# First GRU step's router projection behind the gates, distance rows loaded on SyncE, identity matmuls around the ends' spreading

## The chip, the core and the metric

The kernel runs on one core of a Trainium2 chip. The core has TensorE (PE, matmuls into PSUM), VectorE (DVE), ScalarE (ACT), GpSimd (POOL) and SyncE (SP, which here only issues transfers), each with its own instruction stream; they meet through semaphores. Sixteen DMA engines move data. The metric is the device time of one launch in microseconds, all four stages of the block together.

## What is computed

A block of four sublayers over `x` (32 batches, 100 rows, 256 features) with a context of 32 x 361 x 256, each added to `x` through a gate:

```python
x = x + tanh(g_xattn[0]) * cross_attention(layernorm(x), ctx)
x = x + tanh(g_ffn[0])   * gru_routed_mixture(layernorm(x))
x = x + tanh(g_xattn[1]) * align(ctx, layernorm(x))
x = x + tanh(g_ffn[1])   * capacity_experts(layernorm(x))
```

The change touches the second and the third. In the second a GRU of state width 1024 runs over the 100 rows of each batch, and its states route each row to experts; beside it a projection `expr` of the inputs is needed for the router's scores:

```python
def step(h, xw_t):
    xr, xz, xn = split(xw_t, 3); hr, hz, hn = split(h @ gru_w_hh.T, 3)
    r = sigmoid(xr + hr); z = sigmoid(xz + hz)
    n = tanh(xn + r * hn)
    return (1 - z) * n + z * h
expr = hidden_states @ expr_w.T
```

In the third each batch gets the Euclidean distances of its 100 normalized rows to its 361 context rows, a dynamic time warping over them, the path back, and for each row of `x` the sum of the context rows on the path:

```python
D = sqrt(maximum(aa + bb - 2 * a @ b.T, 0))
R = dtw_cost(D); i_idx, j_idx, valid = backtrack(R)
out = zeros.at[j_idx].add(small[i_idx] * valid)
```

## The kernel before

The order of every engine's work is written out by hand: each engine has a block of code per stage, and an engine's instructions run in the order in which they are written. Semaphore waits (`wait_ge`) stand in the engine's own stream, so whatever is queued behind one waits too.

**The GRU (`gru`).** All 32 batches advance together, 100 steps in 25 tiles of four (`STEPS`); the state is kept as 128 partitions (four quarters of the features by 32 batches). TensorE's step, from L1048 on: input parts of the gates (L1053, into `ps_rz`) and of the candidate (L1058, into `ps_x`), two transposes of the state (L1062), then for the quarter `j` of the tile the router projection (L1064 to L1071, weights `we`, into `ps_e`), then the recurrent gate matmuls (L1076, which need the turned state, copied to `stateT` by VectorE at L999 and ScalarE at L1028) and the recurrent candidate matmuls (L1081). Between the transposes and the gate matmuls the projection covers the copies. Each f32 matmul is two passes in the trace, hence 64 records for 32 matmuls. The weights `we` (1 MB) are loaded by SyncE at the stage's start (L964).

**The distances (`distances`).** Loop over 32 batches, groups of four for the rows' statistics. SyncE loads the first four batches' rows of `x` in two halves and then the contexts `ctxT[b]` (363 KB each) into a ring of eight buffers; from the ninth on it waits until the buffer's squares and distances are done. ScalarE waits for the second half of the first rows, issues the other seven row loads (L1866), and then starts with the square root of the first group's variances (`root_of(0)`, L1852). In its loop it squares context `b`, takes the root for the next group, squares row `b`, and takes the root of distance `b - 2`. VectorE: statistics (L1891 to L1896), reciprocal (L1901), normalized rows (L1907), then per batch `take_x` (L1912), at every fourth batch the statistics of the next group, the rows two batches ahead, and the distance of two batches ago (L1917). GpSimd adds the two halves of the squares. TensorE transposes the rows (L1950) and does three matmuls for each batch. After the loop the distances are placed into `table`.

**The ends (`align`).** VectorE finds the path in `DSTEPS` = 106 steps of two instructions (L2193, L2198), each raising the semaphore `own`. TensorE stands still through this. When `own` is at its end it spreads the path's ends of group 0 and group 1 over the partitions (`spread_ends`, four matmuls each, L2392). ScalarE copies each group out (L2352), VectorE makes three pick tables of each (L2208, L2211, `pick_ready`), and the loop over groups follows: TensorE waits for the picks, spreads group `g + 2`, and selects for each batch with three matmuls (L2428) into `ps_e[b % 3]`; VectorE adds each result to `rows` (L2216). `fill_tensor_engine` (L209 to L212) issues matmuls of the identity whose results nobody reads; the kernel before has seven of them at L2448 and seven at L2542.

## Time and profile before

| | us |
|---|---|
| median of 3 runs | 3206.34 (3204.51 to 3207.49) |
| the profiled execution | 3209.85 |
| its span in the trace | 3208.1 |
| TensorE busy | 2880.4 (90%) |
| VectorE, ScalarE, GpSimd busy | 1310.6, 827.8, 811.1 |
| GRU, first instruction of step 0 to the last state | about 650 to 2080 |
| distances | 2587 to 2691 |
| forward and backward pass of the path | to 2885.8 |

The profile is one execution. A timeline row gives the start, the time from the first start to the last end of like instructions in a row, the engine, the line, output and inputs, and in brackets how long the engine had been idle before and what ended that. TensorE's granted clock is given per stretch as a share of 2.4 GHz; its two levels are 1.0 (2.4 GHz) and 0.5 (1.2 GHz). Times in the trace count from the start of the span.

### The profile page before, as it was taken

Reading aid. Unit: us, or ns where it says so; the run is one execution under the profiler, and the core shown is the slowest. Engines: PE = TensorE matmul, PEld = TensorE weight load, DVE = VectorE, ACT = ScalarE, POOL = GpSimd, SP = SyncE. Lnnn points to the kernel's source line nnn. Section 1 sums busy time; section 2 is a strip of 40 time slices with the busy share of each in tenths; the row PEclk is TensorE's granted clock in tenths of the full one; section 3 lists DMA queues with packets and bytes.
Section 4 is the critical chain, followed back from the end, with each engine's and each line's share of the span. In section 5 each row is a group of like instructions: output and inputs, shape, how many; then the busy total and the mean of one; then the engine's idle time right before and its main releaser. Section 6 shows DMA issues by size and latency. Waiting matters only on the chain. (4 is left out here: it accounts for less than half of the span.)

```text
span 3208.1 us, 70894 instructions
## 1 busy us (share of the span) xinstructions
PE 2880.4 (90%) x29244; PEld 1559.8 (49%) x29245; DVE 1310.6 (41%) x2655; ACT 827.8 (26%) x2170; POOL 811.1 (25%) x759
## 2 busy tenths in 40 slices
PE   7999999899999999999999999999999974009898
PEld 4566666534444444444444444478566643007555
DVE  5655555613332323323323233264222256986311
ACT  3444444411111111111111111121222246471111
POOL 2111111002222222222222222234444431004243
PEclk9999999999999999999999999999999988559899
DMA  7000100220000000000000000051222263005143
GB/s 239 30 26 26 32 26 26 71 81 23 18 23 18 19 22 18 23 17 21 19 18 25 16 24 16 18 205 47 43 45 45 44 175 98 0 1 206 52 116 75
DMA packets 78391, 164.11 MB, mean 51 GB/s; under 512 B 11788, under 2 KB 51568, under 8 KB 73111
## 3 DMA queue, kind: packets, MB, share of 16 engines
q1 hardware_dynamic: 53588, 104.04, 10.4%
q0 software_dynamic: 21456, 40.57, 5.7%
q10 hardware_dynamic: 3074, 15.45, 1.3%
q8 instruction: 223, 3.65, 0.5%
q14 instruction: 50, 0.40, 0.0%
HBM read 119.63 MB, written 40.37 MB: 50 GB/s over the span
## 5 line engine op out<-in xcount | busy, mean ns | idle before, releaser
L1076 PE MATMUL gru_ps_rz<-whh,scratch 128*32 128x512 f32 x6400 | 709.3, 595 | 0.0
L871 POOL TENSOR_TENSOR scratch<-scratch 128x1024 f32<-128x1024 f32 (+3 forms) x246 | 369.5, 1527 | 818.8 <-DVE stat L885 656.5
L1076 PEld LDWEIGHTS gru_ps_rz<-whh,scratch 128*32 128x32 f32 x6400 | 197.9, 110 | 454.1 <-issue 454.1
L1081 PE MATMUL gru_ps_n<-whh,scratch 128*32 128x256 f32 x6400 | 363.6, 379 | 0.0
L1005 DVE TENSOR_TENSOR scratch<-scratch,state 128x256 f32<-128x256 f32 x100 | 52.2, 522 | 667.4 <-ACT scratch L1034 667.4
L1081 PEld LDWEIGHTS gru_ps_n<-whh,scratch 128*32 128x32 f32 x6400 | 207.7, 110 | 180.2 <-issue 59.9
L467 DVE TENSOR_REDUCE att_neg_max<-att_banks 100x2 f32<-100x722 f32 x256 | 221.1, 906 | 122.6 <-PE att_banks L701 122.6
L1034 ACT ACTIVATE scratch<-gru_ps_rz 128x512 f32<-128x512 f32 x100 | 59.7, 597 | 726.7 <-PE gru_ps_rz L1076 726.7
L390 ACT ACTIVATE att_probsT<-att_banks 121x600 f32<-121x600 f32 x256 | 154.3, 672 | 216.7 <-PE att_banks L744 216.7
L1053 PE MATMUL gru_ps_rz<-wih,scratch 128*32 128x512 f32 x1600 | 191.7, 597 | 1.7 <-POOL scratch L973 1.7
L2392 PE MATMUL e_ps_g<-align_reach,ident 32*121 32x101 f32 x64 | 10.9, 326 | 197.0 <-DVE align_reach L2198 195.5
L885 DVE TENSOR_REDUCE stat<-scratch 128x2048 f32 (+3 forms) x96 | 181.1, 1886 | 0.0
L1007 DVE TENSOR_TENSOR scratch<-scratch,gru_ps_n 128x256 f32<-128x256 f32 x100 | 42.1, 421 | 230.3 <-PE gru_ps_n L1081 230.3
L1037 ACT ACTIVATE scratch<-scratch 128x256 f32<-128x256 f32 x100 | 41.7, 417 | 349.0 <-DVE scratch L1009 349.0
L355 POOL DMA_DIRECT2D x<-rows_x x31 | 17.3, 559 | 418.9 <-DVE rows_x L493 418.9
L701 PE MATMUL att_banks<-att_kT,att_qT 32*100 32x361 f32 x1024 | 111.9, 506 | 9.5 <-ACT att_probsT L390 9.1
L744 PE MATMUL att_banks<-att_q_less,att_kT 32*121 32x100 f32 x3072 | 108.7, 277 | 10.8 <-DVE att_neg_max L467 9.5
L1622 DVE COPY mix_room<-mix_ps_m 128x512 f32<-128x512 f32 x57 | 39.4, 692 | 187.7 <-PE mix_ps_m L1711 187.7
L1297 POOL DMA_INDIRECT x<-mix_room,mix_rows_listed x57 | 90.4, 1585 | 90.6 <-ACT mix_room L1357 87.8
L744 PEld LDWEIGHTS att_banks<-att_q_less,att_kT 32*121 32x121 f32 x3072 | 93.6, 179 | 35.9 <-issue 25.0
L1703 PE MATMUL mix_ps_g<-whh,mix_room 128*128 x228 | 107.3, 593 | 2.3 <-ACT mix_room L1351 2.3
L1717 PE MATMUL mix_ps_y<-whh,mix_room 128*128 x456 | 108.0, 380 | 1.0 <-DVE mix_room L1622 1.0
(400 smaller groups left out, 4237.8 us busy)
## 6 DMA issues: line engine op xcount, KB each, us to landing
table<-in_w SPq DMA_DIRECT2D x16, 1024.0 KB, 6.9
states<-state SPq DMA_DIRECT2D x100, 128.0 KB
scratch<-states SPq DMA_DIRECT2D x25, 512.0 KB, 3.5
whh<-in_whhT POOLq DMA_DIRECT2D x8, 1536.0 KB, 19.9
att_c_in<-in_ctxT SPq DMA_DIRECT2D x32, 363.0 KB, 3.2
dist_ctx<-in_ctxT SPq DMA_DIRECT2D x32, 363.0 KB, 4.6
align_ctx<-in_ctx_rows SPq DMA_DIRECT2D x32, 363.0 KB
whh<-in_guT ACTq DMA_DIRECT2D x8, 1024.0 KB, 12.3
```

The source lines that it names most:

```text
L390: nc.scalar.activation(probsT[(HG * b + c) % RING][:, 2 * h:2 * h + 2, :], pair(TURNED, c, h)[0:KC, :, 0:3 * S], ACT.Exp, scale=-1.0).then ...
L467: v_.tensor_reduce(neg_max[0:S, g, :].rearrange("p (r j) -> p r j", j=32)[:, 2 * h:2 * h + 2, HD * (1 - half)], pair(SCORES, c, h)[0:S, :, ...
L701: done = nc.tensor.matmul(banks[0:S, bank_of(SCORES, c, r), 0:KV], qT[b % 2][strip(r), half, g, :], kT[b % 2][strip(r), half, g, 0:KV], st ...
L744: done = nc.tensor.matmul(banks[0:KC, bank_of(TURNED, c, r), m * S:(m + 1) * S], kT[b % 2][strip(r), half, g, m * KC:(m + 1) * KC], q_less ...
L871: done = nc.gpsimd.tensor_tensor(last.prod[:, row:row + rows, :], a, b, ALU.mult)
L885: nc.vector.tensor_reduce(stat[:, bass.ds(it, 1), at:at + rows].rearrange("p a n -> p (a n)"), last.prod[:, 0:rows, :], AX.X, ALU.add).the ...
L1053: nc.tensor.matmul(ps_rz[quarter(q), :], xt[u][:, k, j, :], rz_columns(wih, k, q), start=(k == 0), stop=False)
L1076: last = nc.tensor.matmul(ps_rz[quarter(q), :], stateT[c % 2][:, quarter(c // 2)], rz_columns(whh, c, q), start=False, stop=(c == GC - 1))
L1081: last = nc.tensor.matmul(ps_n[quarter(q), 0:GQ], stateT[c % 2][:, quarter(c // 2)], n_columns(whh, c, q), start=(c == 0), stop=(c == GC - 1))
L1297: nc.gpsimd.indirect_dma_start(x2, bass.IndirectOffsetOnAxis(ap=rows_listed[:, n:n + 1], axis=0), y[u], None, compute_op=ALU.add).then_inc ...
L1703: done = nc.tensor.matmul(psum[:, :], xT[u][:, k, :], experts_w[:, bass.ds(e, 1), k * 2 * FF + half * FF:k * 2 * FF + (half + 1) * FF].rea ...
L1717: done = nc.tensor.matmul(ps_y[:, 0:DIM], midT[:, c, :], experts_w[:, bass.ds(e, 1), GU + c * DIM:GU + (c + 1) * DIM].rearrange("p a n -> ...
```

## The change

Three edits, and no change in what is computed.

1. In the GRU the router projection moves into a helper `project_routed`. It is called where it stood in every step but the very first (`t == 0`); there it is called behind the recurrent gate matmuls.
2. In the distances SyncE issues all row loads, each for a group of four batches: group 0 ahead of the contexts, group `g` behind context `2g - 1`. ScalarE issues none and does not wait for the first rows; it runs a root of one column of `ones` into `warm` at its start, which loads the table of the root. VectorE waits for each group's single load.
3. In `align` TensorE waits until `own` is 16 short of its end (eight steps of two), runs four identity matmuls into `ps_e[2]`, then spreads groups 0 and 1, and runs four more.

```diff
@@ -1043,6 +1043,16 @@
             pe.wait_ge(whh_in, 16 * GC)
             pe.wait_ge(wih_in, 16)
 
+            def project_routed(it, u, j):
+                if j == 0:
+                    pe.wait_ge(we_in, 16)
+                if j % 2 == 0:
+                    pe.wait_ge(e_copied, 2 * it)
+                for k in range(KT):
+                    last = nc.tensor.matmul(ps_e[j // 2][:, (j % 2) * GQ:(j % 2 + 1) * GQ], xt[u][:, k, :, :].rearrange("p j b -> p (j b)"),
+                                            we[:, k, j * GQ:(j + 1) * GQ], start=(k == 0), stop=(k == KT - 1))
+                last.then_inc(e_done, 1)
+
             def steps(it, u):
                 pe.wait_ge(xt_ready, it + 1)
                 for j in range(STEPS):
@@ -1061,14 +1071,8 @@
                     for half in range(2):
                         nc.tensor.transpose(ps_t[half][:, 0:P], h[j % 2][:, half * P:(half + 1) * P], ident[:, :]).then_inc(turned, 1)
 
-                    if j == 0:
-                        pe.wait_ge(we_in, 16)
-                    if j % 2 == 0:
-                        pe.wait_ge(e_copied, 2 * it)
-                    for k in range(KT):
-                        last = nc.tensor.matmul(ps_e[j // 2][:, (j % 2) * GQ:(j % 2 + 1) * GQ], xt[u][:, k, :, :].rearrange("p j b -> p (j b)"),
-                                                we[:, k, j * GQ:(j + 1) * GQ], start=(k == 0), stop=(k == KT - 1))
-                    last.then_inc(e_done, 1)
+                    if t > 0:
+                        project_routed(it, u, j)
                     for half in range(2):
                         pe.wait_ge(stateT_ready[half], t + 1)
                     for c in range(GC):
@@ -1076,6 +1080,8 @@
                             last = nc.tensor.matmul(ps_rz[quarter(q), :], stateT[c % 2][:, quarter(c // 2)], rz_columns(whh, c, q),
                                                     start=False, stop=(c == GC - 1))
                     last.then_inc(rz_done, 1)
+                    if t == 0:
+                        project_routed(it, u, j)
                     for c in range(GC):
                         for q in range(4):
                             last = nc.tensor.matmul(ps_n[quarter(q), 0:GQ], stateT[c % 2][:, quarter(c // 2)], n_columns(whh, c, q),
@@ -1802,13 +1808,13 @@
         ps_d = [ps(f"ps_d{u}") for u in range(RING)]
 
         rows_in = [sem(f"rows_in{g}") for g in range(GROUPS)]
-        first_in = [sem(f"first_in{u}") for u in range(2)]
         ctx_in = [sem(f"ctx_in{u}") for u in range(CTX)]
         padded, squared, added = sem("padded"), sem("squared"), sem("added")
         stats_done, aggregated, root_in, root_out, scaled = (sem("stats_done"), sem("aggregated"), sem("root_in"), sem("root_out"),
                                                              sem("scaled"))
         xn_ready, turned, xT_ready, norm_ready = sem("xn_ready"), sem("turned"), sem("xT_ready"), sem("norm_ready")
         ones_done, summed, square_ready, dist_ready = sem("ones_done"), sem("summed"), sem("square_ready"), sem("dist_ready")
+        warm, warmed = sb("warm", [S, 1]), sem("warmed")
         far_set, placed, taken = sem("far_set"), sem("placed"), [sem("taken_act"), sem("taken_dve")]
         block = ctx.enter_context(nc.Block())
 
@@ -1822,13 +1828,18 @@
 
         @block.sync
         def _(sp):
-            for some, arrived in ((slice(0, 2), first_in[0]), (slice(2, GROUP), first_in[1])):
-                sp.dma_start(rows[:, some, :], x_rows[:, some, :]).then_inc(arrived, 16)
+            def load_rows(g):
+                some = slice(GROUP * g, GROUP * g + GROUP)
+                sp.dma_start(rows[:, some, :], x_rows[:, some, :]).then_inc(rows_in[g], 16)
+
+            load_rows(0)
             for b in range(B):
                 if b >= CTX:
                     sp.wait_ge(squared, b - CTX + 1)
                     sp.wait_ge(summed, b - CTX + 1)
                 sp.dma_start(c_in[b % CTX][:], ctxT[b]).then_inc(ctx_in[b % CTX], 16)
+                if b % 2 and b // 2 + 1 < GROUPS:
+                    load_rows(b // 2 + 1)
 
         @block.gpsimd
         def _(pool):
@@ -1860,10 +1871,8 @@
                 act.wait_ge(square_ready, b + 1)
                 nc.scalar.activation(dist[:, b, 0:KV], dist[:, b, 0:KV], ACT.Sqrt).then_inc(dist_ready, 1)
 
-            act.wait_ge(first_in[1], 16)
-            for g in range(1, GROUPS):
-                some = slice(GROUP * g, GROUP * g + GROUP)
-                act.dma_start(rows[:, some, :], x_rows[:, some, :]).then_inc(rows_in[g], 16)
+            nc.scalar.activation(warm[:], ones[0:S, 0:1], ACT.Sqrt).then_inc(warmed, 1)
+            act.wait_ge(warmed, 1)
             root_of(0)
             for b in range(B + LEAD):
                 if b < B:
@@ -1883,11 +1892,8 @@
 
             def stats_of(g):
                 some = slice(GROUP * g, GROUP * g + GROUP)
-                if g > 0:
-                    dve.wait_ge(rows_in[g], 16)
+                dve.wait_ge(rows_in[g], 16)
                 for b in range(GROUP * g, GROUP * g + GROUP):
-                    if g == 0:
-                        dve.wait_ge(first_in[b // 2], 16)
                     v.bn_stats(stats[:, b, :], rows[:, b, :]).then_inc(stats_done, 1)
                 for b in range(GROUP * g, GROUP * g + GROUP):
                     dve.wait_ge(stats_done, b + 1)
@@ -2413,8 +2419,11 @@
                                             start=(k == 0), stop=(k == KT - 1))
                 done.then_inc(scored, 1)
 
+            pe.wait_ge(own, POINTERS + 2 * DSTEPS - 16)
+            fill_tensor_engine(nc, ps_e[2], ident, 4)
             spread_ends(0)
             spread_ends(1)
+            fill_tensor_engine(nc, ps_e[2], ident, 4)
             for g in range(GROUPS):
                 pe.wait_ge(pick_ready, 3 * g + 3)
                 if g + 2 < GROUPS:
```

In the order of TensorE, start of the GRU (`gru_ps_rz` holds the gates, `gru_ps_e` the projection, `gru_ps_n` the candidate); a name of the kernel before comes first. Before:

```order
L1053 MATMUL gru_ps_rz<-wih,scratch 32x512 x8
L1058 MATMUL gru_ps_x<-wih,scratch 32x256 x8
L1062 MATMUL gru_ps_t<-ident,state 128x128 x2
L1069 MATMUL gru_ps_e<-gru_we,scratch 128x256 x2
L1076 MATMUL gru_ps_rz<-whh,scratch 32x512 x32
L1081 MATMUL gru_ps_n<-whh,scratch 32x256 x32
L1053 MATMUL gru_ps_rz<-wih,scratch 32x512 x8
L1058 MATMUL gru_ps_x<-wih,scratch 32x256 x8
```

and after:

```order
L1063 MATMUL gru_ps_rz<-wih,scratch 32x512 x8
L1068 MATMUL gru_ps_x<-wih,scratch 32x256 x8
L1072 MATMUL gru_ps_t<-ident,state 128x128 x2
L1080 MATMUL gru_ps_rz<-whh,scratch 32x512 x32
L1052 MATMUL gru_ps_e<-gru_we,scratch 128x256 x2
L1087 MATMUL gru_ps_n<-whh,scratch 32x256 x32
L1063 MATMUL gru_ps_rz<-wih,scratch 32x512 x8
L1068 MATMUL gru_ps_x<-wih,scratch 32x256 x8
```

In the first step the two projection matmuls now stand between gates and candidate; the second step is as before.

ScalarE at the start of the distances (`dist_rstd` is the variance that becomes the reciprocal root), before:

```order
L1866 DMA rows<-x 100x1024 x7
L1852 ACT_TABLE_LOAD
L1852 ACTIVATE dist_rstd<-dist_rstd 100x4
L1847 ACTIVATE dist_square<-dist_ctx 128x722
L1852 ACTIVATE dist_rstd<-dist_rstd 100x4
L1857 ACTIVATE dist_xx,dist_norm<-dist_xn 100x256
```

and after:

```order
L1874 ACT_TABLE_LOAD
L1874 ACTIVATE dist_warm<-ones 100x1
L1863 ACTIVATE dist_rstd<-dist_rstd 100x4
L1858 ACTIVATE dist_square<-dist_ctx 128x722
L1863 ACTIVATE dist_rstd<-dist_rstd 100x4
L1868 ACTIVATE dist_xx,dist_norm<-dist_xn 100x256
```

The seven issues are gone and the table load stands at the start, ahead of the first root.

SyncE at the same place, before:

```order
L1823 UNCONDITIONAL_BRANCH
L1826 DMA rows<-x 100x512 x2
L1831 DMA dist_ctx<-in_ctxT 128x726 x32
L1780 UNCONDITIONAL_BRANCH
L2128 UNCONDITIONAL_BRANCH
```

and after:

```order
L1833 DMA rows<-x 100x1024
L1840 DMA dist_ctx<-in_ctxT 128x726 x2
L1833 DMA rows<-x 100x1024
L1840 DMA dist_ctx<-in_ctxT 128x726 x2
L1833 DMA rows<-x 100x1024
L1840 DMA dist_ctx<-in_ctxT 128x726 x2
L1833 DMA rows<-x 100x1024
```

One row load of four batches now stands behind each second context, up to eight in all.

TensorE around the ends (`e_ps_g` takes the spread ends, `e_ps` the selections), before:

```order
L1979 MATMUL dist_ps_x<-ident,dist_all 32x100 x364
L1780 UNCONDITIONAL_BRANCH
L2381 UNCONDITIONAL_BRANCH
L2392 MATMUL e_ps_g<-align_reach,ident 121x101 x12
L2428 MATMUL e_ps<-align_ctx,align_cost 100x256 x12
L2392 MATMUL e_ps_g<-align_reach,ident 121x101 x4
```

and after:

```order
L1985 MATMUL dist_ps_x<-ident,dist_all 32x100 x364
L1786 UNCONDITIONAL_BRANCH
L2387 UNCONDITIONAL_BRANCH
L212 MATMUL e_ps<-ident 128x512 x4
L2398 MATMUL e_ps_g<-align_reach,ident 121x101 x8
L212 MATMUL e_ps<-ident 128x512 x4
L2398 MATMUL e_ps_g<-align_reach,ident 121x101 x4
L2437 MATMUL e_ps<-align_ctx,align_cost 100x256 x12
```

Four identity matmuls now stand ahead of the first eight spreads, and four between these and the spread of group 2.

## Rows read from the trace of the kernel before

**Rows 1.** The page, busy time of the engines over the span.

```profile
PE 2880.4 (90%) x29244; PEld 1559.8 (49%) x29245; DVE 1310.6 (41%) x2655; ACT 827.8 (26%) x2170; POOL 811.1 (25%) x759
```

**Rows 2.** Timeline, GRU step 0: start us, us, engine, line, what [idle <-releaser].

```profile
655.38 0.27 ACT L1028 COPY scratch<-gru_ps_t 128x128 f32<-128x128 f32 x1 [7.03 <-PE gru_ps_t L1062]
...
658.58 2.07 PE L1069 MATMUL gru_ps_e<-gru_we,scratch 128*128 128x256 f32 x4 [3.23 <-DMA gru_we<-in_weT]
660.58 8.98 PE L1076 MATMUL gru_ps_rz<-whh,scratch 128*32 128x512 f32 x64
669.39 3.63 PE L1081 MATMUL gru_ps_n<-whh,scratch 128*32 128x256 f32 x64
...
675.80 1.03 PE L1069 MATMUL gru_ps_e<-gru_we,scratch 128*128 128x256 f32 x4
676.76 7.07 PE L1076 MATMUL gru_ps_rz<-whh,scratch 128*32 128x512 f32 x64
```

**Rows 3.** Windows, step 0: stretch, us, PE busy, granted clock, DMA share, GB/s.

```profile
656.00:658.00 2.00, 0.00 (x0) 0.91 0.87 340
...
664.00:666.00 2.00, 2.00 (x24) 0.88 0.00 0
```

**Rows 4.** Timeline, all engines, start of the distances.

```profile
2591.22 3.76 ACTq L1866 DMA_DIRECT2D rows<-x  x7
2591.22 0.75 DVE L1891 BATCH_NORM_STATS2 dist_stats<-rows 100x6 f32<-100x256 f32 x2 [0.42 <-DMA rows<-x]
...
2595.01 1.28 ACT L1852 ACT_TABLE_LOAD   x1 [14.23 <-issue]
...
2596.54 0.18 DVE L1901 RECIPROCAL dist_rstd<-dist_rstd 100x4 f32<-100x4 f32 x1 [4.08 <-ACT dist_rstd L1852]
...
2597.86 0.37 DVE L1912 TENSOR_SCALAR dist_xT<-dist_ps_x 128x200 f32<-128x200 f32 x1 [0.37 <-PE dist_ps_x L1950]
2600.56 1.40 DVE L1891 BATCH_NORM_STATS2 dist_stats<-rows 100x6 f32<-100x256 f32 x4 [2.33 <-DMA rows<-x]
```

**Rows 5.** Context loads and squares of all; the third load; DMA queues 2600 to 2602.

```profile
L1847 ACT ACTIVATE dist_square<-dist_ctx x32: 788/790/794, 2596.4 to 2664.0; 128x722 f32<-128x722 f32 x32
...
L1831 SPq DMA_DIRECT2D dist_ctx<-in_ctxT x1: 427/427/427, 2588.9 to 2588.9; - x1
...
DMA to landing us min/median/max: 6.3/6.3/6.3
...
q10 hardware_dynamic: 67, 0.25, 37.1%
q1 hardware_dynamic: 70, 0.19, 27.9%
```

**Rows 6.** Timeline, all engines, around the ends' spreading.

```profile
2880.33 0.32 DVE L2193 SCALAR_TENSOR_TENSOR align_masked<-align_place,align_reach,table 128x91 f16<-128x91 f16 x1
...
2885.86 3.57 PE L2392 MATMUL e_ps_g<-align_reach,ident 32*121 32x101 f32 x16 [195.52 <-DVE align_reach L2198]
2887.84 0.50 ACT L2352 CAST align_ends<-e_ps_g 121x404 f16<-121x404 f32 x1 [2.73 <-PE e_ps_g L2392]
...
2890.95 1.94 PE L2392 MATMUL e_ps_g<-align_reach,ident 32*121 32x101 f32 x8 [1.53 <-DVE align_cost L2211]
...
2900.12 1.08 PE L2392 MATMUL e_ps_g<-align_reach,ident 32*121 32x101 f32 x8
2900.23 0.48 DVE L2216 SCALAR_TENSOR_TENSOR rows<-e_ps,gate_x,rows 100x256 f32<-100x256 f32 x1 [0.48 <-PE e_ps L2428]
...
2901.14 4.13 PE L2428 MATMUL e_ps<-align_ctx,align_cost 121*100 121x256 f32 x18
```

**Rows 7.** The later fill: matmuls, weight loads, and a window with the granted clock.

```profile
2978.48 8.07 PE L212 MATMUL e_ps_g<-ident 128*128 128x512 f32 x14
...
2979.47 0.34 PEld L212 LDWEIGHTS e_ps_g<-ident 128*128 128x128 f32 x1 [0.52 <-issue]
...
2982.00:2983.00 1.00, 1.00 (x4) 0.94 0.00 0
```

## The prediction

> **What bounds the kernel now.** TensorE is busy for 90% of the span [rows 1], so the first question for each edit is whether TensorE, or what it waits for, is late at that place. I read the timeline of the first GRU step, then of the start of the distances, then of the stretch in which the path's ends are spread, with the granted clock beside each. All three are single passages, run once, in a chain where each stage starts when the one ahead has ended. Time taken out of one is taken out of the kernel unless a later wait holds an absolute time; I found none: the later waits are on work of the same chain and move with it.
>
> **Part 1, the first GRU step.** Before, TensorE turns the state, and the next thing in its queue is the router projection, which needs the weights `we`. It sits idle for 3.23 us until their DMA lands at 658.58 [rows 2]. The turned state had been ready from 655.38 + 0.27 = 655.65 on. The granted clock had come up to full by then, falls during the idle time (0.91 over 656 to 658) and is back only in 664 to 666 [rows 3]. So the wait costs twice: the projection takes 2.07 us instead of the 1.03 of the next step, and the 64 recurrent gate passes 8.98 instead of 7.07 [rows 2].
> With the projection behind the gate matmuls of step 0 only, these start when the state is there, about 0.35 us after TensorE went idle:
> - idle time: 3.23 - 0.35 = 2.9 us less;
> - gate matmuls at full clock: 8.98 - 7.07 = 1.9 us less;
> - the projection is still run, at full clock and behind the gates: 2.07 - 1.03 = 1.0 us less. By 662.8 its weights have long landed (658.58).
> Sum 5.8 us. What is late next? The sigmoids start when the gates end and now have the projection and the candidate matmuls (1.0 + 3.5 us) as cover instead of 3.5 alone, so they hold nobody. The copy of the projection is taken in step 2 and is far off. From the end of the candidate matmuls on the step is as before. The bounds: 2.9 us if the clock falls or rises late all the same (the idle time alone), 5.8 with the clock up. I take 5.8, since the 0.35 us of idle that stays is about what TensorE shows in every later step with its clock up.
>
> **Part 2, the start of the distances.** Before, ScalarE waits for both halves of the first rows (2591.22), then issues seven row loads (3.76 us), then loads the root's table at 2595.01 (1.28 us), and only then takes the root that VectorE needs at 2596.54 [rows 4]. After, VectorE waits for one load of the four first batches. Its end I put where the second half landed, 2591.22. Four statistics (1.40), then aggregation and the epsilon (about 0.35 more, an estimate: they are shorter than the statistics and overlap them in part), root (0.2) with hand-overs (0.1): the reciprocal at 2593.2, that is 3.3 us earlier. The table load lies at the stage's start at 2587.3, where ScalarE has nothing else. But what holds the stage is the next wait: VectorE has taken batch 0 at 2597.86 + 0.37 and then stands until the second group of rows lands, at 2600.56 [rows 4]; everything behind follows from that moment. After, it would be there at 2598.23 - 3.3 = 2594.9. So the gain is decided by when the second group lands, now the fourth transfer of SyncE's queue, behind the first rows and contexts 0 and 1, instead of the first of ScalarE's, issued at 2591.22.
> Its landing time: the third context, issued at 2588.9, landed 6.3 us later, at 2595.2 [rows 5], behind 0.40 MB of rows and with 3 x 0.363 MB of contexts. In 2600 to 2602, with transfers outstanding in both queues, these took only 37.1 + 27.9 = 65% of the 16 DMA engines' time [rows 5]. So something like a third of the engines have no part in the rows' transfers, and I count each 0.40 MB of rows as 0.615 MB. Then 0.615 + 1.09 = 1.70 MB had landed at 2595.2. I put the first packets at 2588.5, 1.2 us after SyncE's first issue at the stage's start, and 1.4 us for the completion (both estimates; the one row load whose issue and landing the rows bound, 2587.3 to 2591.22, leaves room for them), so the rate is 1.70 / 5.3 = 0.32 MB/us. The second group ends at 2 x 0.615 + 2 x 0.363 = 1.96 MB, or 6.1 us: 2588.5 + 1.4 + 6.1 = 2596.0. With plain bytes (1.53 MB against 1.49) it would be 2595.3. I take 2596.2: 4.3 us gained. Bounds: 5.6 if VectorE itself is last (2594.9), 3.3 if the landing slips to 2597.3.
> The Trainium skill (page "DMA: Bandwidth & Descriptors", section "Why a DMA increments its semaphore by 16 and not by 1") says that a transfer over 100 partitions is put on 10 of the 16 engines, one over 128 on all. The 65% above agrees. With that page's figure of about 27 GiB/s for an engine the four transfers would take an estimated 4.3 us and land before 2594.9, which would make this part 5.6 us and the time 3192.7; the landing of 6.3 us measured here says that the engines are slower than that.
> SyncE then queues eight more issues than before, each some 0.4 us, without a wait up to context 7; that is far ahead of their use.
>
> **Part 3, around the ends.** Before, the spreads of groups 0 and 1 run at half clock: 16 passes in 3.57 us from 2885.86, where eight later ones take 1.08 [rows 6]. After, four identity matmuls are released eight VectorE steps before the path's end, at 2880.35 (the row at 2880.33 is the first of the eight). A matmul here is two passes, each 0.34 + 0.52 = 0.86 us at half clock; in the fill of seven at 2978.48 the clock came up 3.6 us after its start, and the passes took half of that from there [rows 7]. So: 3.6 us for 4.2 passes, then 3.8 x 0.43 = 1.6, end at 2885.6, just ahead of the path's end at 2885.86. Then at full clock: two spreads 2 x 1.02 = 2.0 (2887.9), the second fill 8 x 0.43 = 3.4 (2891.35), third spread 1.0 (2892.4). The second fill is in the way: the picks would release the third spread at 2890.95 - 0.85 = 2890.1, so it costs 1.2 us. Then four selections at (4.13 / 3) each = 5.4 us with the hand-over: the fourth result is added at 2897.8 instead of 2900.23 [rows 6]. Gain 2.4 us. VectorE is busy without a break from that addition on (statistics, then the picks of group 2), so this shift carries. If the clock comes up only after 5.5 us the first fill ends 0.7 late: 1.7 us. I take 2.2; bounds -1 and 3.5.
>
> **Sum.** 5.8 + 4.3 + 2.2 = 12.3 us. The profiled execution took 3209.85 us (span 3208.1), 3.5 above the median of the three runs; it gives 3197.6 for the same execution, and the median 3206.34 - 12.3 = **3194.0 us**.
>
> **Rivals.**
> - *The clock is no gain in the GRU step* (it falls, or rises late, also without the wait). Against it: the clock is still at 0.91 on average over 656 to 658 after the wait has begun, and only 0.35 us of idle is left. Part 1 is 2.9: 3196.9. Chance 0.12.
> - *The fills are in the way.* The clock stays low through both: first fill 6.9 us (2887.25), spreads 3.4, second fill 6.9, third spread 1.9, four selections as before 7.4: 2906.8 instead of 2900.23, 6.6 lost. Gain 10.1 - 6.6 = 3.5: 3202.8. Against it: fills brought the clock up within 3.6 us. Chance 0.04; for part 3 at about zero (3196.2) another 0.1.
> - *The row loads starve the contexts*, on the other side. Context 15 is needed at 2632.0 before (the last of the 32 squares at 2664.0, and 2.0 us for each one ahead of it, a little under the mean of (2664.0 - 2596.4) / 31 = 2.2 with the slow start in it [rows 5]), 2627.7 after. Ahead of its end SyncE's queue then holds all rows: 8 x 0.615 + 16 x 0.363 = 10.7 MB. At 0.32 MB/us that is there at 2623.2, 4.5 us to spare. At 0.25 it comes at 2632.7 and takes back 5.0 (3199.0, chance 0.06). From 0.215 MB/us down it costs more than the 12.3 us of all three parts; at 0.18 it comes at 2649.3, 21.6 late: 3194.0 + 21.6 = 3215.6. For it: all loads now share one queue, and rows crowd on part of the engines. Against it: the rate measured at the start. Chance 0.02.
> - *The change does less than it says*: the second rows land as late as 2600, since contexts and rows interleave. Part 2 is then 0.5: 3197.8. Chance 0.06.
>
> **How the numbers follow.** My forecast has 0.6. Of the rivals those at 3196 to 3199 hold 0.34 and stay faster; 0.04 for two of them at once, taken out of that, the low clock through the fills (0.04) lie within 0.2%. The low end: 5.8 + 5.6 + 3.5 = 14.9, or 3191.4, and 1.5 us for the spread of the median: 3190. The high end takes in one rival of the larger kind, 3200. Range **3190 to 3200**. A measurement of this kernel can tell about 0.2%, 6.4 us, from no change, so the line of "faster" is 3199.9: faster 0.90, same 0.08, slower 0.02.
>
> **What would show it.** Step 0: gate matmuls start near 655.7, take 7.1 us, and no idle time waits for `we`. Distances: reciprocal some 6 us after the stage's start, the second group's statistics 8.9 us after it instead of 13.3, and a steady 2.0 us per batch behind, with no wait on a context. Ends: clock up at the first spread, the fourth addition some 12 us after the path's end instead of 14.4, and the third spread waiting for the fill rather than for the picks. The forecast is wrong if the clock is low in the gates of step 0, if squares wait for contexts, or if the fills are still at half clock when the path ends.

## The result, and the profile after

| | before | changed |
|---|---|---|
| median of 11 runs each | 3206.97 us (3203.97 to 3216.10) | 3199.68 us (3193.61 to 3202.51) |
| ratio | | 0.9974, 95% interval 0.9965 to 0.9983 |
| the profiled execution, its span | 3209.85, 3208.1 | 3199.82, 3198.1 |

The changed kernel is faster by 5.5 to 11 us, 8.3 by the ratio, where I had forecast 12.3. Two later comparisons of the same two kernels gave 0.9963 (0.9950 to 0.9977) and 0.9965 (0.9952 to 0.9977), 11 to 12 us. So the direction and the range held, the range in the first comparison by 0.3 us (3199.68 against its end at 3200); the medians of the later two are 3194.94 and 3195.69 us. The question is where the difference to 12.3 sits.

The first GRU step, TensorE's timeline of the changed kernel (start and duration in us, engine, line, operation, out<-in, count, and in brackets the idle time ahead of it with what ended it), against [rows 2]:

```profile
649.54 3.33 PE L1063 MATMUL gru_ps_rz<-wih,scratch 128*32 128x512 f32 x16 [1.73 <-POOL scratch L973]
...
654.56 7.08 PE L1080 MATMUL gru_ps_rz<-whh,scratch 128*32 128x512 f32 x64 [0.45 <-ACT scratch L1028]
661.56 1.13 PE L1052 MATMUL gru_ps_e<-gru_we,scratch 128*128 128x256 f32 x4
662.62 3.66 PE L1087 MATMUL gru_ps_n<-whh,scratch 128*32 128x256 f32 x64
666.10 1.90 PE L1063 MATMUL gru_ps_rz<-wih,scratch 128*32 128x512 f32 x16
```

The wait for `we` is gone, the gates take 7.08 us instead of 8.98, the projection 1.13 instead of 2.07. From the step's first matmul to that of the next step it is 16.56 us, before 22.6.

The start of the distances, all engines, against [rows 4]:

```profile
2584.39 1.28 ACT L1874 ACT_TABLE_LOAD   x1 [6.68 <-PEq L1107]
...
2589.34 1.41 DVE L1897 BATCH_NORM_STATS2 dist_stats<-rows 100x6 f32<-100x256 f32 x4 [14.37 <-DMA rows<-x]
...
2591.56 0.18 DVE L1907 RECIPROCAL dist_rstd<-dist_rstd 100x4 f32<-100x4 f32 x1 [0.33 <-ACT dist_rstd L1863]
...
2592.87 0.37 DVE L1918 TENSOR_SCALAR dist_xT<-dist_ps_x 128x200 f32<-128x200 f32 x1 [0.37 <-PE dist_ps_x L1956]
2593.91 1.41 DVE L1897 BATCH_NORM_STATS2 dist_stats<-rows 100x6 f32<-100x256 f32 x4 [0.67 <-DMA rows<-x]
```

The stage starts at 2584.39. The table load lies in idle time, the reciprocal comes 7.2 us after the start, and the second group's statistics 9.52 us after it, before 13.28. The last wait there is still the landing of those rows (0.67 us of idle).

Around the path's ends, TensorE, against [rows 6]:

```profile
2877.52 2.09 PE L212 MATMUL e_ps<-ident 128*128 128x512 f32 x4
2879.54 1.93 PE L2398 MATMUL e_ps_g<-align_reach,ident 32*121 32x101 f32 x16
2881.40 3.71 PE L212 MATMUL e_ps<-ident 128*128 128x512 f32 x8
2885.05 1.08 PE L2398 MATMUL e_ps_g<-align_reach,ident 32*121 32x101 f32 x8
```

Both spreads together take 1.93 us instead of 3.57, the second fill ends as the third spread starts, and from the path's end (2879.41) to the fourth addition it is 12.1 us instead of 14.4.

So each passage shows what the prediction named, with sizes that are compared with it further down. What I had not looked for stands elsewhere. At the first expert tile of the mixture, 1590 us behind the GRU's first step and in code that the change doesn't touch, TensorE in the changed kernel shows

```profile
2240.35 3.78 PE L1709 MATMUL mix_ps_g<-whh,mix_room 128*128 x4 [1.62 <-ACT mix_room L1357]
```

and in the kernel before

```profile
2246.44 1.98 PE L1703 MATMUL mix_ps_g<-whh,mix_room 128*128 x4 [1.79 <-ACT mix_room L1351]
```

The windows of TensorE show what the clock did (stretch, its length, TensorE busy and its matmuls, the granted clock, the DMA share, GB/s); first the changed kernel, then the one before at the same work:

```profile
2238.00:2240.00 2.00, 0.41 (x2) 0.91 0.45 131
2240.00:2242.00 2.00, 1.65 (x2) 0.50 0.15 35
2242.00:2244.00 2.00, 2.00 (x4) 0.50 0.08 31
2244.00:2246.00 2.00, 2.00 (x4) 0.50 0.00 0
2246.00:2248.00 2.00, 1.45 (x5) 0.88 0.00 0
```

```profile
2244.00:2246.00 2.00, 0.41 (x2) 1.00 0.47 131
2246.00:2248.00 2.00, 1.56 (x4) 1.00 0.13 29
2248.00:2250.00 2.00, 2.00 (x6) 1.00 0.10 37
```

Both have the same pauses of TensorE there, between the shared expert's last matmuls and the first gates. Before, the clock stays at 2.4 GHz through them; after, it falls to 1.2 GHz and comes back some 7 us later. The tile takes 13.49 us instead of 10.63: 2.9 us given back.

### The profile page after: what moved, and what is told of

Same layout as the page of the kernel before. It is cut to its first block and busy times, and to the rows that moved or that the text cites. A ratio compares the mean times of both kernels' runs of the same rounds, so it can differ in the third digit from the quotient of the medians.

```text
span 3198.1 us, 70927 instructions
## 1 busy us (share of the span) xinstructions
PE 2887.9 (90%) x29260; PEld 1563.9 (49%) x29261; DVE 1309.8 (41%) x2655; ACT 828.2 (26%) x2171; POOL 811.7 (25%) x759
## 5 line engine op out<-in xcount | busy, mean ns | idle before, releaser
L212 PE MATMUL e_ps<-ident 128*128 128x512 f32 x16 | 9.4, 739 | 190.1 <-DVE align_reach L2204 190.1
L1037 ACT ACTIVATE scratch<-scratch 128x256 f32<-128x256 f32 x100 | 41.7, 417 | 350.3 <-DVE scratch L1009 350.3
## 6 DMA issues: line engine op xcount, KB each, us to landing
whh<-in_guT ACTq DMA_DIRECT2D x8, 1024.0 KB, 12.3
```

## The experiments

Behind the first two runs twelve more were made, so there are 14 traces of ten different kernels (three of the changed kernel, two each of the kernel before and of the GRU part alone). Each passage of the table is measured between the same two instructions in every trace. "GRU 0": first input matmul of step 0 to that of step 1. "Tile": from the transposing of the first expert tile's tokens to that of the third tile's, which takes in all matmuls of the first tile's gate and up projections. "Distances": the stage's start to the first matmul that places distances in the table. "Ends": the path's end to the fourth addition. "Tail": the last addition to the capacity stage's first expert matmul. "From GRU": first input matmul to the end. All in us.

| kernel | GRU 0 | tile | distances | ends | tail | from GRU | timed ratio (95%) |
|---|---|---|---|---|---|---|---|
| before | 22.61 | 10.63 | 82.56 | 14.43 | 46.91 | 2557.9 | |
| b2_before_again | 22.48 | 10.60 | 82.32 | 14.73 | 46.33 | 2556.6 | |
| changed | 16.55 | 13.49 | 79.52 | 12.12 | 46.33 | 2548.6 | 0.9974 (0.9965, 0.9983) |
| a2_after_again | 16.65 | 13.67 | 78.12 | 12.86 | 46.12 | 2548.5 | 0.9963 (0.9950, 0.9977) |
| a3_after_again | 17.45 | 12.18 | 79.38 | 12.10 | 46.42 | 2547.6 | 0.9965 (0.9952, 0.9977) |
| e1_gru | 16.69 | 11.89 | 82.40 | 14.22 | 48.37 | 2555.0 | 0.9993 (0.9984, 1.0002) |
| e4_gru_again | 17.06 | 12.27 | 82.80 | 14.85 | 44.47 | 2554.4 | |
| e2_dist | 22.88 | 10.53 | 79.54 | 15.44 | 46.34 | 2557.1 | 0.9990 (0.9980, 1.0000) |
| e3_ends | 22.43 | 10.60 | 82.78 | 12.03 | 41.51 | 2552.9 | 0.9990 (0.9981, 0.9999) |
| w1_warm_tile | 16.60 | 10.28 | 79.09 | 12.04 | 48.37 | 2548.3 | 0.9959 (0.9948, 0.9971) |
| f1_first_fill_only | 17.47 | 10.42 | 78.77 | 13.93 | 46.31 | 2547.0 | 0.9977 (0.9967, 0.9987) |
| d1_rows_earlier | 16.72 | 13.60 | 80.33 | 12.04 | 46.39 | 2549.5 | 0.9964 (0.9951, 0.9977) |
| g1_fill_in_wait | 20.06 | 10.56 | 82.35 | 15.08 | 46.24 | 2553.7 | |
| k1_tail_fill | 17.52 | 10.28 | 78.27 | 13.16 | 42.89 | 2544.3 | 0.9963 (0.9949, 0.9977) |

One thing about the time itself: the first input matmul of the GRU starts at 645.7 to 653.3 us in these 14 traces, and the code ahead of it is the same in all. So a single execution's total says little about a change of this size; "from GRU" leaves that part out.

### Each part alone: e1_gru, e2_dist, e3_ends, and the changed kernel again

The edits are the three pieces of the change, each put into the kernel before by itself. e1_gru (the helper and the call that it replaces are as in the change):

```diff
+                    if t > 0:
+                        project_routed(it, u, j)
...
+                    if t == 0:
+                        project_routed(it, u, j)
```

e2_dist has all lines of `distances`; e3_ends:

```diff
+            pe.wait_ge(own, POINTERS + 2 * DSTEPS - 16)
+            fill_tensor_engine(nc, ps_e[2], ident, 4)
             spread_ends(0)
             spread_ends(1)
+            fill_tensor_engine(nc, ps_e[2], ident, 4)
```

> The kernel before with the first edit alone: in GRU step 0 the router projection stands behind the gate matmuls. Theory A (the prediction's sum holds, part by part): 5.8 us less in the median, since both the idle time and the low clock go in every execution. Theory B (the profiled execution of before was an unlucky one: whether TensorE's clock falls in the wait for the projection's weights differs between executions): 3 to 4 us less in the median; in this run's own trace the gate matmuls of step 0 still start about 1 us after the transposes and take about 7.1 us. Theory C (time gained in the GRU is lost again at the start of the mixture's expert tiles, because the change moves them): the first expert tile shows the gate matmuls at half clock (3.8 us instead of 2.0) in this kernel too.

> The kernel before with the second edit alone: all row loads on SyncE and the root's table early. Theory A: the second group's statistics start about 9.0 to 9.5 us after SyncE's first issue of the stage, instead of 13.3, and nothing behind gives it back: 3.8 us less. Theory B (the loads through one queue take some of it back further on): under 2 us less from the stage's start to the first path step, with squares that wait for contexts between batch 4 and 16. Theory C (clock luck elsewhere): the median moves by another amount than the trace's stage does, by up to 3 us either way.

> The kernel before with the third edit alone: four identity matmuls ahead of the spreads and four behind. Theory A: the fourth result is added about 12.1 us after the path's end instead of 14.4, and the median is 2.2 us less. Theory B (the clock comes up only late in the fills in a good part of the executions): 0.5 to 1.5 us less in the median, and the first spread starts up to 1.4 us after the path's end. Theory C: same or slower, the fills delay more than they give.

> The changed kernel as it is, again, for a second trace of the same kernel on the same chip as the single edits. Theory A (12.3 us by three additive parts): the ratio comes out near 0.9962, and the three single edits add up to it. Theory B (the profiles of before and after are single draws, and TensorE's clock falls and rises at other moments in each execution): the ratio stays near 0.9974 (8 us), and this trace shows the first expert tile of the mixture without the half-clock stretch that the first trace of this kernel had (gate matmuls 2.0 instead of 3.8 us).

Measured medians: 3204.42, 3203.66 and 3203.36 us for the three parts beside 3207.53 for the kernel before, and 3194.94 for the changed kernel. By the ratios the parts are worth 2.2, 3.2 and 3.2 us, 8.6 together, each with an interval of about 3 us to either side; the whole of it 11.9. The timing can't tell more from it than that each part's best value is a gain; for the GRU part the interval still takes in no change, and for the distances it ends at none. Of the theories for the changed kernel again, the ratio of 0.9963 is that of Theory A, and the first expert tile is at half clock in its second trace too (13.67 us), against Theory B; that the single edits add up to the whole can't be told with such intervals.

The traces can. Each passage shrinks in just those kernels that have its part: GRU 0 from 22.6 to 16.7, distances from 82.5 to 79.5, ends from 14.4 to 12.0. In e2_dist the second group's statistics start 10.23 us after the stage's start, later than the 9.0 to 9.5 that I expected, and the stage is 3.0 us shorter all the same. And the first tile is at 11.89 us in e1_gru, at 10.53 and 10.60 in the other two. So far the fall of the clock there came along with the GRU part. The other two edits lie behind the tile and can't bring it.

### Work in the pause: w1_warm_tile

```diff
+            fill_tensor_engine(nc, ps_r, ident, 1)
             turn_x(0, 0, 16)
+            fill_tensor_engine(nc, ps_r, ident, 2)
             turn_of(0, 0, expert_of(0), after=False)
```

> The changed kernel with three more identity matmuls on TensorE around the turning of the first expert tile's tokens in the mixture (one ahead of it, two behind it), at the place where the three kernels with the change in the first GRU step showed TensorE's clock at 0.50 and 13.49, 13.67 and 11.89 us for the first tile, and the three without it 10.63, 10.53 and 10.60. Theory C (the fall of the clock in that pause is a cost that the change in the first GRU step brings with it, and it is caused by the idle time of TensorE there): with work in the pause the first tile takes about 10.6 us again, the clock is at full in the gate matmuls behind it (1.9 us for four instead of 3.8), and the kernel is about 3 us faster than the changed one: near 3192, ratio about 0.995. Rival L (the fall there is chance, three of three by luck, and the time missing from my sum lies elsewhere): the time is that of the changed kernel, 3195 to 3199.7, or up to 1 us more for the three matmuls. Rival S (the clock falls whatever stands in so short a pause): the first tile takes 13.5 us plus up to 1.3 for the added matmuls at full or 2.6 at half clock.

```profile
2241.19 1.13 PE L212 MATMUL mix_ps_r<-ident 128*128 128x512 f32 x2 [0.58 <-DVE mix_room L1582]
2242.16 0.38 PE L1704 MATMUL mix_ps_x<-ident,mix_room 128*128 128x128 f32 x2
2242.38 1.89 PE L212 MATMUL mix_ps_r<-ident 128*128 128x512 f32 x4
2244.11 1.88 PE L1709 MATMUL mix_ps_g<-whh,mix_room 128*128 x4
```

TensorE's timeline of w1_warm_tile: the added matmuls stand where it was idle, the gates take 1.88 us, the tile 10.28 us, and so again in k1_tail_fill, which has the same matmuls. Rival S is out. Whether it is 3 us of time is not shown: 3194.75 us (ratio 0.9959) beside 0.9963 to 0.9974 of the changed kernel, with intervals that overlap. In its trace the 3.2 us of the tile are there, but the tail is 2.0 us longer than in the changed kernel, so that "from GRU" stays where it was. That the pause is where the clock is lost, and that work in it keeps the clock up, holds; the 3 us of time, and whether the GRU part brings the fall, stay open here.

### The two fills: f1_first_fill_only

The changed kernel without its second fill:

```diff
             spread_ends(1)
-            fill_tensor_engine(nc, ps_e[2], ident, 4)
```

> The changed kernel without its second fill (the four identity matmuls between the second and the third spread of the path's ends); the first fill stays. In the changed kernel that second fill took 3.71 us and the third spread started 5.5 us after the first, while the picks had ended 1.3 us before it. Theory A (the second fill costs what it delays, and the clock holds without it): third spread about 4.2 us after the first instead of 5.5, the selections behind it at full clock (1.36 us for each group of six), the fourth addition 1.3 us earlier, and the kernel 1.3 us faster. Theory B (the second fill is what keeps the clock up through the pause of some 2.3 us): the third spread starts 1.3 us earlier, but TensorE's clock falls, the selections take up to 2 us more, and the fourth addition is 0.5 to 1 us later than in the changed kernel.

```profile
2876.41 1.93 PE L2398 MATMUL e_ps_g<-align_reach,ident 32*121 32x101 f32 x16
2880.65 1.94 PE L2398 MATMUL e_ps_g<-align_reach,ident 32*121 32x101 f32 x8 [2.31 <-DVE align_cost L2217]
2882.52 6.98 PE L2436 MATMUL e_ps<-align_ctx,align_cost 121*100 121x256 f32 x24
```

```profile
2876.00:2878.00 2.00, 2.00 (x17) 1.00 0.00 0
2878.00:2880.00 2.00, 0.34 (x4) 0.72 0.03 8
2880.00:2882.00 2.00, 1.35 (x7) 0.50 0.00 0
```

TensorE's timeline and windows of f1_first_fill_only. The third spread starts 4.24 us after the first instead of 5.50, as both theories have it. But TensorE is idle for 2.31 us ahead of it, the clock falls in that time, the spread takes 1.94 us instead of 1.08 and the selections 6.98 instead of 5.42. The fourth addition comes 13.93 us after the path's end, against 12.1, 12.9 and 12.1 in the three traces of the changed kernel. Part of that is the first fill, which in f1_first_fill_only ends late, so that the first spread starts 0.79 us after the path's end. Counted from the first spread, the fourth addition comes after 13.14 us, and after 11.98 or 11.99 in all seven traces with both fills: 1.2 us later. Theory B. The second fill costs 1.3 us of delay and saves 2.4; the prediction priced the first half of that and not the second.

### The order in SyncE's queue: d1_rows_earlier

```diff
-                if b % 2 and b // 2 + 1 < GROUPS:
+                if b % 2 == 0 and b // 2 + 1 < GROUPS:
```

> The changed kernel with each later group of rows one context earlier in SyncE's queue: the second group stands behind context 0 instead of behind context 1. In the changed kernel VectorE still waited 0.67 us for that group at the stage's start (its statistics began at 9.52 and 8.79 us after the stage's start in two traces). Theory A (the landing follows from the bytes ahead of it in the queue): the second group lands about 1.1 us earlier (0.363 MB at 0.32 MB per us), VectorE no longer waits for it, its statistics start about 8.8 us after the stage's start, when VectorE has taken batch 0, and context 1 is late by at most 1.9 us, which shows as a wait of the square of batch 1 or not at all. Rival R (that transfer shares the 16 engines with all that is outstanding, and its place in the queue matters little): no change beyond the 0.7 us by which the two traces of the changed kernel differ.

The second group's statistics start 8.35 us after the stage's start, right behind the taking of batch 0, with no wait: Theory A for the landing. Still the stage is longer, 80.33 us to the first placing against 78.1 to 79.5. Of ScalarE's waits in the stage (engine, line, what for, us in total, times, longest) these are the long ones that matter:

```profile
ACT dist_rstd L1863 <- DVE dist_rstd L1902: 11.7, 6, 5.0
ACT dist_all L1872 <- DVE dist_all L1923: 9.3, 17, 2.0
...
ACT dist_square L1858 <- DMA dist_ctx<-in_ctxT: 5.9, 6, 2.0
```

In the first and third trace of the changed kernel the last of these doesn't exist: no square waits for its context. In its second trace there is a little of it, in batches 12 and 14:

```profile
ACT dist_square L1858 <- DMA dist_ctx<-in_ctxT: 0.9, 2, 0.6
```

With all row loads one context earlier, squares wait six times, 5.9 us in all, in batches 7 to 13:

```profile
2615.86 0.81 ACT L1858 ACTIVATE dist_square<-dist_ctx 128x722 f32<-128x722 f32 x1 [1.97 <-DMA dist_ctx<-in_ctxT]
```

That is my rival "the row loads starve the contexts", on a small scale. Already the order that was chosen touches it in one trace of three, without a longer stage (78.12 us, the shortest), and one context earlier it costs time. There is little room: over 10 us from 9.6 us after the stage's start on, and the two times 10 us behind that, the DMA engines are busy for 81, 90 and 87% in the changed kernel, and in the same stretches of the kernel before for 71, 91 and 73%. The context behind the early rows, context 1, landed 9.1 us after the stage's start, 2.2 to 2.7 us later than in the three traces of the changed kernel, where I had expected 1.9 at most. It is one trace, so the 1.3 us by which the stage is longer (0.8 to 2.2 against single traces) has no interval of its own.

### The clock without the order: g1_fill_in_wait, and before again

The kernel before with work in its wait for `we`:

```diff
+        ps_fill = ps("ps_fill")
...
+                    if t == 0:
+                        fill_tensor_engine(nc, ps_fill, ident, 4)
                     if j == 0:
                         pe.wait_ge(we_in, 16)
```

> The kernel before with four identity matmuls on TensorE, into a PSUM bank that nothing else uses, in step 0's wait for the weights `we`; the order of the router projection and the gate matmuls stays as before. It takes the two parts of my 5.8 us for the GRU step apart. If the clock fell because TensorE had nothing to do in that wait: the gate matmuls of step 0 take 7.1 us instead of 8.98 and 9.08, the projection 1.03 instead of 2.07, and they start no earlier than before (9.9 to 10.4 us after the first input matmul), so the passage of 22.6 us up to step 1 shrinks to about 19.7. If the order was what mattered: 22.6 us stay. On the first expert tile: if the fall of the clock there in the kernels with the projection behind the gates came from the clock's history in step 0, this one takes over 12 us too; if it came from anything else, 10.6 us as in the four traces without that part.

> The kernel before, unchanged, for a second trace of it. If the readings on which the prediction and the verdict rest are properties of the kernel, they come again: 8.98 us for the gate matmuls of step 0, 22.6 us from the first input matmul to that of step 1, 10.6 us for the first expert tile with the clock at full, 13.3 us from the start of the distances to the statistics of the second group, 14.4 us from the path's end to the fourth addition, and about 46.9 us for the routing tail. If the first tile takes over 12 us here, the fall of the clock there has nothing to do with the change in the first GRU step.

```profile
652.54 0.44 PE L1063 MATMUL gru_ps_t<-ident,state 128*128 128x128 f32 x2
652.82 3.61 PE L212 MATMUL gru_ps_fill<-ident 128*128 128x512 f32 x8
656.27 1.02 PE L1072 MATMUL gru_ps_e<-gru_we,scratch 128*128 128x256 f32 x4
657.22 7.07 PE L1079 MATMUL gru_ps_rz<-whh,scratch 128*32 128x512 f32 x64
```

TensorE's timeline of g1_fill_in_wait: gates at 7.07, projection at 1.02, GRU 0 at 20.06 us against 22.61 and 22.48. So of the 5.1 to 6.0 us that the GRU part takes off, about 2.5 are had by keeping TensorE busy: 3.0 in the projection and the gates, less about 0.4 by which the projection starts behind the landing of its weights, since the fill still runs. The remaining 3 or so are the wait itself. In this trace the clock follows TensorE's idle time and not the order. The second trace of the kernel before repeats the first in all passages within 0.6 us.

The tile is at 10.56 us here: the clock staying up in step 0 did not by itself bring the fall at the tile.

### Is the fall at the tile chance? e4_gru_again, a3_after_again

> The kernel before with the GRU part of the change alone, unchanged from e1_gru, for a second trace. By the theory that the GRU part brings the fall of the clock at the first expert tile: over 11.8 us for that tile again (13.5, or 11.9). By chance alone: 10.6 us is as likely. In step 0: 16.7 us to step 1 again.

> The changed kernel, unchanged, on the same chip and beside the same runs of the kernel before as k1_tail_fill, and a third trace of it. If the gains in the three passages are properties of the kernel they come again: 16.6 us to step 1, 8.8 to 9.5 us to the statistics of the second row group, 12.0 to 12.9 from the path's end to the fourth addition. The time should lie between the two medians so far, 3194.9 and 3199.7. The first expert tile took over 11.8 us in four of five traces of kernels with its GRU part (13.49, 13.67, 11.89, 13.60, and 10.42 in one) and 10.5 to 10.6 in all four without it: by the theory that this part brings the fall with it, over 11.8 us here too; a value of 10.6 makes it two of six and leaves chance open.

The tile takes 12.27 and 12.18 us, both over the 11.8 of the theory. Of the seven traces with the GRU part and nothing added at the tile, six show the fall (11.9 to 13.7 us) and one, f1_first_fill_only, does not (10.42). Of the five without that part none does (10.53 to 10.63). Were the fall as likely in both kinds, six falls among twelve traces would all lie in those seven in 7 of 924 ways.

That count makes it look surer than it is, because the two kinds of traces differ in one more thing, which the edit can't have caused. TensorE's clock comes up 2.9 to 3.2 us after step 0's first input matmul in the changed kernel's first trace, a2_after_again, e1_gru and d1_rows_earlier (and w1_warm_tile), and 3.9 to 4.9 us after it in all the others, though everything up to there is the same code. In those five the clock is also low for some 10 us behind the GRU instead of 7, and in the first four it is 0.7 to 0.8 us further from step 1 to the first tile than in the kernel before. These four show the fall; w1_warm_tile, with work in the pause, doesn't. No trace of a kernel without the GRU part had such a start. Among the traces with the other kind of start the fall came in two of three with the part (12.18 and 12.27, against 10.42 in the third) and in none of five without, and that would happen by chance in 3 of 28 ways. So the fall goes with the part in these traces, and chance is not excluded.

In step 0 the two runs took 17.06 and 17.45 us to step 1 where I expected 16.7 and 16.6: the input matmuls ran at half clock for longer, the gates took 7.07 us as before. The second group's statistics came after 9.02 us and the fourth addition after 12.10, as expected, and the median of 3195.69 lies between the two earlier ones. How a step that ends 1580 us earlier could matter at the tile no run shows: the clock is at full from the end of step 0 to the last GRU step in all of them, and none moves the pause alone. That stays open.

### The routing tail: k1_tail_fill

w1_warm_tile, and ten instead of seven matmuls in the fill ahead of the 64 slot matmuls:

```diff
-            fill_tensor_engine(nc, ps_g[0], ident, 7)
+            fill_tensor_engine(nc, ps_g[0], ident, 10)
             pe.wait_ge(places_ready, 1)
```

> The changed kernel with the three identity matmuls around the first expert tile (as in w1_warm_tile) and ten instead of seven identity matmuls in the fill of the routing tail, which stands ahead of the 64 narrow matmuls that sum the slots. In nine of ten traces so far these 64 run at half clock, 10.4 to 10.6 us, after 1.9 us of idle; in e3_ends, where only 0.71 us of idle lay ahead of them, at full, in 5.84. Theory A (what the tail pays is that idle time): the fill ends at about the moment the slots are released, they take some 5.9 us, the tail from the last addition to the capacity stage shrinks from 46.1 to 48.4 us to about 41.7, and the kernel is 3 to 5 us faster than w1_warm_tile: about 3191. Rival B (e3_ends was lucky, and the narrow matmuls let the clock fall themselves): they take 10.5 us, and the fill, if it ends late, adds up to 1.3 us.

```profile
2971.72 10.88 PE L212 MATMUL e_ps_g<-ident 128*128 128x512 f32 x20
2982.44 5.79 PE L2465 MATMUL e_ps<-align_cost 100*100 100x64 f32 x64
```

TensorE's timeline of k1_tail_fill, and the same slot matmuls in w1_warm_tile and in e3_ends:

```profile
2980.00 10.56 PE L2465 MATMUL e_ps<-align_cost 100*100 100x64 f32 x64 [1.92 <-DVE align_cost L2336]
```

```profile
2987.36 5.84 PE L2457 MATMUL e_ps<-align_cost 100*100 100x64 f32 x64 [0.71 <-DVE align_cost L2328]
```

The expectation's "10.4 to 10.6 in nine of ten" and its idle time of 1.9 us are wrong. The 14 traces make a ladder of idle time ahead and duration: 0 and 5.79; 0.71 and 5.84; 0.92 and 8.76; 1.06 and 9.02; 1.19 and 9.25; 1.31 to 1.35 and 9.47 to 9.55 (four traces); 1.55 and 9.90; 1.58 and 9.95; 1.83 and 10.40; 1.92 and 10.56 (two). For the slots Theory A holds in its one trace: with no idle time ahead, full clock. The tail is 42.9 us (forecast 41.7), 3.2 to 5.5 less than in the other traces of the changed kernel and its variants, and "from GRU", at 2544.3, is the lowest of all. The median of six runs, 3196.86 us, is no lower than the changed kernel's 3195.69 beside the same runs of before. One trace shows the gain; the timing doesn't, and the three or four us are the size of the spread of these medians. It is no version that I can call better.

## Why the prediction was right or wrong

**Part 1, 5.8 us.** Measured on the mean of three traces of the changed kernel (16.88) against two of before (22.55): 5.7. Gates started 5.0 to 5.9 us after the step's first matmul, I had 655.7 - 650.23 = 5.5; they took 7.07 us as forecast. The split in idle time, 2.9, and clock, 2.9, came out as about 3 and 2.5 in g1_fill_in_wait, or 3.0 for the clock without what the fill itself costs. The rival "the clock is no gain" is refuted: in all nine traces with the GRU part the gates take 7.07 us, in the four without it and without a fill 8.98 to 9.18. One reason that I gave was a misreading: from step 1 on TensorE's timeline shows no idle time ahead of the gates, so later steps were no evidence that a short idle time is harmless. The clock held through 0.45 us of it all the same.

**Part 2, 4.3 us.** Measured 3.4 (82.44 against 79.01). The mechanism was right, the landing a little early: the statistics of the second group start 8.8 to 9.5 us after the stage's start in the three traces of the changed kernel, forecast 8.9, and at up to 10.2 in the four others with this order. The first group's rows were later than I had them, 4.3 to 5.0 us after the start (forecast 3.9), so the reciprocal stood at 6.5 to 7.2 instead of 6; the wait behind it hid this. SyncE has six issues more than before and not eight, which changes nothing in the sum.

In all three traces of the changed kernel VectorE still waited 0.57 to 0.67 us for these rows. The Trainium skill (page "DMA: Bandwidth & Descriptors", section "Why a DMA increments its semaphore by 16 and not by 1") has 10 engines for a transfer of 100 partitions. With the figure for an engine in the table "Specifications" of the same page of the Trainium skill, the prediction's estimate put the landing ahead of the moment at which VectorE is free. The landing came behind that moment, so the rate measured in the trace of before was the better guide here.

Over all 13 traces but d1_rows_earlier the statistics start 13.1 us after the stage's start with the old order (six traces) and 9.3 with the new (seven), which is 3.8, and the first placing comes 82.5 and 79.0 us after it, which is 3.6. So most of what is missing to 4.3 is the landing, which was 0.4 us later than forecast, and a base that was high: the trace of before, with 13.28, was above the mean. "Everything behind follows from that moment" holds on average within 0.3 us: from the statistics to the first placing it is 68.9 to 70.0 us with the old order and 69.0 to 70.4 with the new. Single traces differ by more. In the first trace of the changed kernel the fifth square starts 2.58 us after the fourth instead of 2.00, and ScalarE's step ahead of it waited 0.99 us for VectorE's distance. The same delay stands in e4_gru_again (2.62), which has the old order, so it is not of this change; that it hangs on when TensorE's clock comes up is argued, and no run isolates it. The rival of the starved contexts showed in a small way: two short waits in one trace of three, and six in d1_rows_earlier, one context away. Its check by bytes left out that context 8 and all behind it are issued only when a buffer is free.

**Part 3, 2.2 us.** Measured 2.2 (14.58 against 12.36). Two steps of its working were off. The first fill ended 0.1 to 0.9 us behind the path's end in the changed kernel (up to 1.2 in k1_tail_fill), where I had 0.3 ahead. This is all by which the passage varies: counted from the first spread, the fourth addition comes after 11.98 or 11.99 us in all seven traces with both fills. And the second fill, which I booked as a cost of 1.2 us, is what keeps the selections at full clock (f1_first_fill_only), so without it the gain would have been smaller and not larger.

**The sum.** 5.7 + 3.4 + 2.2 = 11.3 us against 12.3. The step that failed is the one before all parts: "Time taken out of one is taken out of the kernel unless a later wait holds an absolute time; I found none." No wait held it, but the clock did. The first tile gives back 13.1 - 10.6 = 2.5 us, a term that the sum lacks. Between step 1 and the first tile another 0.5 us comes back on average, 0.8 in the two traces in which the clock is low for some 10 instead of 7 us behind the GRU. With both, 8.3; the remaining passages agree within 0.4 us each and together give 0.7, and from the GRU's start to the end the traces show (2557.9 + 2556.6) / 2 - 2548.2 = 9.0. The timed differences of 8.3, 11.9 and 11.3 us lie on both sides of it, and their intervals, 5.5 to 16 us together, don't tell 9 from 12.3. So the traces show the missing term, the timing alone doesn't, and that 3199.68 still fell inside the range was a matter of 0.3 us.

**The base.** I noted that the profiled execution was 3.5 us above the median and subtracted from the median, which was right: the part ahead of the GRU alone varies by 7.6 us.

## What to carry to other kernels

Taking idle time out of TensorE's stream pays twice where the clock falls in it, and identity matmuls in a wait get the clock's half of that by themselves; a fill is best read by the idle time left behind it: 0 in k1_tail_fill with the slot matmuls at full clock, 1.1 to 1.9 us in the other traces of the changed kernel and its variants with them slowed. When a passage is made shorter, compare the granted clock in every later pause of TensorE too, since a pause that was harmless in five traces was costly in six of seven, in code that nobody touched. And when loads move to one queue, look one position to either side: here one context earlier brought the rows 0.4 to 1.2 us forward and made the stage about 1.3 us longer, in one trace.

## What the runs showed of the hardware that I had not expected

- The clock fell from 2.4 to 1.2 GHz around an idle time of TensorE of only 2.31 us (f1_first_fill_only, 1.00 ahead of it, 0.50 behind; 0.72 over 2878 to 2880 puts the fall near 2878.9, some 0.5 us after TensorE's last matmul), and did not around one of 1.79 us (before, at the tile). In the tail the 64 slot matmuls ran 5.84 us behind 0.71 us of idle time and 8.76 us behind 0.92. The same pause can go either way from one execution to the next: 10.42 against 13.49 us at the first tile in kernels with the same code there.
- How long the clock took to rise in the first fill of the ends differed as well: its eight passes took 5.67 us in the changed kernel, 6.41 in its second trace, and 5.24 to 6.71 over all eight traces with that fill.

```profile
2871.21 6.41 PE L212 MATMUL e_ps<-ident 128*128 128x512 f32 x8 [190.03 <-DVE align_reach L2204]
```

- Row loads and contexts compete for the DMA engines even where both stand well ahead of their use: one context earlier for each row load made squares wait 5.9 us in total, and 0.9 already in one trace of the order that was chosen.
